# Moving the next chunk's distance behind the first copies in a deformable-convolution kernel

## The reference

```python
def _block(x, dc_w, dc_b, of_w, of_b, dw, db):
    h = relu(_deconv2d(x, dc_w, dc_b))              # 3x3
    offset = _conv2d(h, of_w, of_b, PAD)            # 18 channels: y and x of 9 taps
    return relu(_deform_conv2d(h, offset, dw, db))

def _deform_conv2d(x, offset, w, b):
    py = base_y + offset[:, :, 0]; px = base_x + offset[:, :, 1]
    sampled = bilinear_sample(x, py, px)            # weights 1-|py-yi|, 1-|px-xi|
    return einsum('bckhw,ock->bohw', sampled, w) + b

x = _block(gn(x), ...)            # then three more, each on x + in_prev
x_cat = concatenate((x, in_module), axis=1)         # 64 channels
out = x_in + _deform_conv2d(x_cat, _conv2d(x_cat, fin_off_w, ...), fin_dcn_w, ...)
```

## Time and profile before

| what | value |
|---|---|
| median of 3 runs | 4506.23 us (4501.54 to 4509.08) |
| profiled execution | 4504.67 us, span 4502.9 us |
| busy PE / PEld | 3951.5 us (88%) / 3022.6 us (67%) |
| busy DVE / ACT / POOL | 2921.2 us (65%) / 2777.9 us (62%) / 1143.3 us (25%) |
| mean granted clock of TensorE | 0.918 |
| DMA packets | 527.19 MB, mean 117 GB/s |

### The profile page before, as it was taken

How to read it: one execution, slowest core, us unless ns; L and a number is a source line. 1 busy time by engine, 2 the same in 40 slices (tenths; PEclk the granted TensorE clock), 3 DMA queues, 4 the chain that set the end, 5 groups by cost and what they waited for, 6 DMA issues and landing times.

```text
span 4502.9 us, 221715 instructions
## 1 busy us (share of the span) xinstructions
PE 3951.5 (88%) x81888; PEld 3022.6 (67%) x81888; DVE 2921.2 (65%) x5838; ACT 2777.9 (62%) x6651; POOL 1143.3 (25%) x655
## 2 busy tenths in 40 slices
PE   5998798799699879979969988986999998799998
PEld 3676576577477657657747765764777776677776
DVE  4785686588478568658847856863666663566665
ACT  2785587488388558748838856872555552455554
POOL 0341243144034124214403413420111110111110
PEclk8999899799899989979979998997999999899999
DMA  3442443344244244334424424436555553655554
GB/s 115 120 125 69 126 125 92 93 125 125 72 121 125 65 122 125 92 102 125 123 69 122 125 67 127 125 104 175 135 138 131 137 133 105 164 134 138 129 138 100
DMA packets 243253, 527.19 MB, mean 117 GB/s; under 512 B 61152, under 2 KB 151776, under 8 KB 225632
## 3 DMA queue, kind: packets, MB, share of 16 engines
q1 hardware_dynamic: 242880, 522.27, 44.6%
HBM read 465.57 MB, written 56.45 MB: 116 GB/s over the span
## 4 chain that ended last, share of the span: by engine, by line
PE 76%; SPq 9%; issue 6%; DMA 3%; ACT 3%; DVE 2%; POOLq 1%; POOL 0%; ACTq 0%; PEld 0%; PEldq 0%; DVEq 0%
PE P L539 30%; PE PS L557 28%; PE PS L570 9%; PE P L510 7%; SPq L395 4%; SPq L387 3%; DMA HB<-off_store 1%; ACT H L816 1%; PE PS L510 1%; ACT YC L752 1%; DVE FOFF L1000 1%; DMA off_store<-FOFF 1%; SPq L377 1%; DVE ST L1004 1%; DVE ST L1003 0%
## 5 line engine op out<-in xcount | busy, mean ns | idle before, releaser
L883 DVE TENSOR_TENSOR A<-P,YC 121x384 f32<-121x384 f32 (+1 forms) x4608 | 2310.6, 549 | 995.2 <-ACT YC L752 847.8
L539 PE MATMUL P<-HL,SEL 32*121 32x384 f16 (+1 forms) x21504 | 1752.2, 306 | 326.0 <-issue 161.5
L752 ACT ACTIVATE YC<-P 121x384 f32<-121x384 f32 (+1 forms) x4608 | 1732.0, 444 | 23.3 <-PE P L539 17.0
L539 PEld LDWEIGHTS P<-HL,SEL 32*121 32x121 f16 (+1 forms) x21504 | 1136.4, 117 | 718.1 <-issue 372.3
L557 PE MATMUL PS<-A,VT 121*32 121x80 f32 (+1 forms) x40960 | 1390.6, 252 | 31.9 <-ACT SMP L729 15.3
L557 PEld LDWEIGHTS PS<-A,VT 121*32 121x32 f32 (+1 forms) x40960 | 1134.3, 118 | 335.9 <-issue 192.7
L1064 POOL CAST HL<-DIST 128x1152 f16<-128x1152 f32 x320 | 365.6, 1143 | 3101.3 <-DVE DIST L888 3008.8
L729 ACT ACTIVATE SMP<-PS 128x480 f32<-128x480 f32 (+3 forms) x1152 | 592.7, 514 | 749.8 <-PE PS L557 744.6
L1066 POOL TENSOR_TENSOR HL<-DIST,HL 128x1152 f16<-128x1152 f32 x320 | 769.3, 2404 | 134.7 <-issue 75.5
L719 ACT ACTIVATE DIST<-HB,CONST 128x1152 f32<-128x1152 f32 x320 | 400.7, 1252 | 424.6 <-DMA HB<-off_store 214.3
L570 PE MATMUL PS<-SMP,CW 128*64 128x128 f32 x7424 | 475.9, 277 | 5.4 <-ACT SMP L729 5.4
(11 more groups left out here) (56 smaller groups left out, 584.0 us busy)
## 6 DMA issues: line engine op xcount, KB each, us to landing
HB<-off_store SPq DMA_DIRECT2D x2560, 72.0 KB
VT<-ht_store SPq DMA_DIRECT2D x256, 512.0 KB
VT<-ht_store SPq DMA_DIRECT2D x768, 132.0 KB
VT<-ht_store SPq DMA_DIRECT2D x256, 88.0 KB
off_store<-FOFF SPq DMA_DIRECT2D x160, 128.0 KB, 2.5
ht_store<-A SPq DMA_DIRECT2D x32, 256.0 KB, 3.3
ht_store<-VT SPq DMA_DIRECT2D x32, 256.0 KB, 3.2
A<-x_dram SPq DMA_DIRECT2D x2, 2048.0 KB, 10.3
```

What stands on the lines that cost most here:

```text
L539: mm = nc.tensor.matmul(dst, SEL[q, table, 0:sh.npos], hats, start=part == 0, stop=part == 1)
L752: nc.scalar.activation(YC[0:sh.npos, g % X_SLOTS, 0:sh.size], P[0:sh.npos, g % Y_SLOTS, 0:sh.size], ACT.Copy).then_inc(y_ready, 1)
L883: return nc.vector.tensor_tensor(dst, x, y, ALU.mult)
```

## The change

ACT made the next chunk's distance at the start of a chunk, before copy 0. Now it makes it behind copy `next_after` of the first batch: behind copy 1, in front of the read of the sum, in the first four layers; behind copy 4, in front of the read of the first part, in the final layer. DVE's clamp follows: it stood behind product 1 and now stands behind product `next_after + 1`, which is 2 or 5. Nothing else is touched.

```diff
+        self.next_after = self.sum_after if self.batches == 1 else self.after[0]
...
                             n = (c * sh.batches + b) * sh.ngr + g
-                            if b == 0 and g == 0 and not last:
-                                next_distance(c + 1, band + half, 1 - half)
                             act.wait_ge(y_full, n + 1)
 
                             act.wait_ge(product_done, n + 1)
                             nc.scalar.activation(YC[0:sh.npos, g % X_SLOTS, 0:sh.size], P[0:sh.npos, g % Y_SLOTS, 0:sh.size],
                                                  ACT.Copy).then_inc(y_ready, 1)
+                            if b == 0 and g == sh.next_after and not last:
+                                next_distance(c + 1, band + half, 1 - half)
...
                             one_product(g, b, half).then_inc(product_done, 1)
-                            if b == 0 and g == 1 and not last:
+                            if b == 0 and g == sh.next_after + 1 and not last:
                                 clamp(c + 1)
```

## The result

| kernel | median, us | lowest to highest | ratio to before, 95% interval |
|---|---|---|---|
| before | 4506.98 (4 runs) | 4501.54 to 4509.08 | |
| after | 4453.18 (4 runs) | 4449.42 to 4458.79 | 0.9876 [0.9864, 0.9887] |

The change takes 54 us where 165 were forecast; 4453 lies above the range (4300 to 4425). The direction was right, and so was the clock: TensorE's mean granted clock rose from 0.918 to 0.939.

A forecast was written before the change was run, and what follows sets the result against it. It took PE's own work as the main bound (three quarters of the chain), plus final-layer stalls for ACT's copy and their clock loss. 4504.67 - 156 (final layer) - 8 (starts) = 4341 us; range 4309 to 4365, with rivals A and B 4300 to 4425.

The forecast's parts named there:

- steady state nothing: First four layers: waiting before spread 4 is exchanged for waiting for POOL at the chunk's head; steady chunks stay 8.58 us.
- The ring: First-layer loop from POOL's end through spreads, copies, distance, product 2 and clamp to POOL's end: 8.58 us, bounds 8.35 and 8.9.
- head: First part of that first-layer loop, POOL's end to distance: 0.15 to PE's spread, 0.6 to copy 0, 0.37 and 0.39 for copies.
- Rival B: First layers: the loop through POOL takes 8.75 us, sum's read or copy 0 late; 41 us lost, 4382 us; chance 0.17.
- Rival A: Final layer: the stall goes, but small pieces keep the lower clock once a chunk; 4423 us; chance 0.12.
- the rule that the prediction cites for it: Trainium skill on TensorE's clock: frequent micro-idles between matmul groups can make it oscillate; final-layer gain then near the smaller bound, 74 us.
- C: First layers: from a loop of about 9.2 us PE stands over 1 us a chunk and the clock falls; 4650 us; chance 0.04.
- D: Final layer: the distance ends behind the part, PE waits for the read, the stall only moves; 4491 us; chance 0.03.
- about 0.55 us of PE's time in small pieces: Final layer: late copy 1 and product 0, needed by x-spread 4, cost PE 0.55 us a chunk, without lowering the clock.
- The starts: Start of each first-layer step: second chunk's first part about a microsecond earlier; -1.0 us a step, times eight, -8 us.
- SP's bound: First layers: SP's DMA issues take 8.69 us a chunk and would hold the chunk there were the loop through POOL shorter.
- a chunk can hardly become faster: First layers: with the loop at 8.58 us and SP's issues at 8.69, chunks can become slower but hardly faster.

The follow-up runs named there:

- residual late: Against after: in the first four layers DVE's addition of the sum to X moved from behind product 3 to behind product 10; 4391.03 us.
- early clamp: Against after: in the first four layers DVE's clamp put back behind product 1, the distance left where the change has it; 4342.69 us.

## Why the prediction was wrong

**The failing step is "steady state nothing" in the first layers.** It was to cost 0 in 240 chunks and cost 0.41 us a chunk: 12.0 us over the 29 chunks behind the second of a step, 96 in eight steps. The second chunk gives back 5 of them and the ends of the steps 4, which leaves the 87 measured. What fell and what stood inside it:

- The ring, from distance to POOL's end, was worked out as 7.07 us; after has 7.05 to 7.17, residual late 7.05 and 7.17. Its head, POOL's end to the distance, was 1.51; residual late has 1.6. Ring 8.7, not 8.58, inside its bounds. This is 0.12 of the 0.41. Rival B had named it (8.75, copy 0 late), and its sign, distances 8.75 and more apart, came; but it was priced at 41 us and knew nothing of the queue.
- The head presumed that PE and ACT stand ready when POOL ends. In after the distance comes 1.87 us behind POOL's end (1328.47 to 1330.34) in one chunk and 2.00 (1337.40 to 1339.40) in the next, since ACT is still at the third part's read and copy 11. That is 0.3 of the 0.41. PE's queue is released by POOL only in every second chunk, and so it was in before already.
- Why they are late: **DVE's queue was not walked behind the moved clamp.** The prediction gave the clamp a place in the ring (0.75) and asked nothing of product 3 and the residual behind it. And the residual's price was not looked up at its new neighbour: beside POOL's cast it takes 1.08 us.

Rival A did not happen: the final layer's clock is 1.00 with 1.1 us a chunk lost in small pieces, so the rule that the prediction cites for it does not hold here. Neither did C, that the ring reaches 9.2 and the clock falls: the chunk reached 9.0 and the clock in the first layers is 1.00. D's condition, the distance ending behind the part, did not come either.

**The final layer: right mechanism, one term too small.** Stall gone, clock back, distance and clamp covered, no wait for the read. Only "about 0.55 us of PE's time in small pieces", with 0.1 for the clamp, was 1.1: the chunk 17.68 for 17.3, 133 us for 156. Chunks of 17.4-17.5 and 17.9-18.0 take turns; the cause of that stays open.

**The starts: right in sign, about half in size.** The second chunk's first part begins 36.1 us behind the step's first distance where it began at 36.6, -0.5 for the "about a microsecond" told, and its last copy comes at 42.8 for 43.5, -0.6 in the mean of eight steps; forecast -1.0, bounds -2.5 and +0.5. Single steps differ by up to 2 us in either kernel, so this is weak evidence. By the fourth chunk the dearer chunks have used the gain up.

**SP's bound: right, and decisive for what could be had.** "SP's 8.69 a chunk stands behind it" is where the early clamp stops: its 8.55 are below SP's 8.69, which the slack left by the first chunks allows, and part of that goes in waits for windows. But "a chunk can hardly become faster" held only for the ring with the clamp behind product 2; with it behind product 1, POOL's end follows the distance by 5.95 us, and with half of the loads the chunk is 7.9.

Of what would show it, the clock, the wait for YC and the missing wait for the read came as told. Distances 8.5 to 8.7 apart did not, nor "SP never waiting": at 9.0 us a chunk SP waits for PE (5.3 us in 15 waits, 1290 to 1480 us). PE's wait for POOL is there in every second chunk, as "issue", but before has it too, so it was no sign.

## What to carry to other kernels

When an operation moves, walk the whole queue of each engine that follows it, the consumer's too: here ACT's own move was free, and a clamp of 0.75 us with an addition behind it on DVE turned the first layers' half into a loss of 87 us, two thirds of what the final layer gained. Where one edit touches two loops with different limits, price it per loop, and keep or mend each part by what it brings. A follower need not move with what it follows: leaving the clamp in the slot where DVE idles anyway was worth 110 us against after, and 30 against changing the final layer alone.

## What the runs showed of the hardware

- The residual, with X and TMP both in SBUF, takes 344 ns alone, 610 in before and 1078 in after, and in the last two ends 0.15 us after POOL's cast (cast 1333.68 to 1334.82, residual 1333.89 to 1334.97; in before the rows below). Started 0.68 us after the cast it loses 0.3, started 0.21 after it 0.7. The products beside POOL's instructions, whose P is in PSUM, keep 0.55. This agrees with the Trainium skill, "SBUF — State Buffer", section "Who interferes with whom": a DVE instruction with two SBUF inputs contends with a GpSimd instruction that reads SBUF, and the port pair that the two share is an exclusive lock. The residual came second each time, and since it ended only 0.15 us after the cast, less than its own 0.34, not all of it waited.

```profile
1303.42 1.14 POOL L1064 CAST HL<-DIST 128x1152 f16<-128x1152 f32 x1 [4.72 <-DVE DIST L888]
...
1304.10 0.61 DVE L877 SCALAR_TENSOR_TENSOR X<-X,CONST,TMP 128x128 f32 x1
```

- An offset load of 144 KB with an outer dimension of two held SP for 1.67 us in the mean (0.63 at least, 336 of 768 over 2 us); two of 72 KB take 0.96 together, from start to start.
- The granted clock fell to the lower level behind 24 of the 28 stands of PE of 1.1 to 1.4 us in the final layer's first group of before (0.93), and behind 20 of 29 stands of 1.1 us with the distance behind copy 0 (0.94). It stayed at 1.00 where 1.1 us a chunk was lost between matmuls. Pieces were priced rightly at nothing for the clock.
